# Unread matmuls in the tail of an attention and expert kernel, and an earlier second input load

## The reference

```python
# layer 1: linear cross-attention, 16 heads of depth 8
q, k, v = (split_heads(layernorm(z @ w) * gamma + beta) for z, w in ((h, wq), (ctx, wk), (ctx, wv)))
q_prime, k_prime = relu(q) + 1e-6, (relu(k) + 1e-6) * mask
kv = einsum('bhnd,bhne->bhde', k_prime, v * mask)
z = 1 / (einsum('bhnd,bhd->bhn', q_prime, k_prime.sum(-2)) + 1e-6)
out = layernorm(einsum('bhnd,bhde,bhn->bhne', q_prime, kv, z) @ dense_w + dense_b) * gamma + beta
# layer 2: causal self-attention (16 heads, softmax), then a mixture of 8 experts, top 2
h = h + attention(layernorm(h) * g1 + b1)
f = layernorm(h) * g2 + b2
w_full = softmax over the two largest of (f @ gate_W + gate_b), 0 elsewhere
h = h + sum_e w_full[:, e] * (gelu(f @ W1[e] + b1[e]) @ W2[e] + b2[e])
```

## Time and profile before

| | us |
|---|---|
| median of 3 runs | 579.07 (576.87 to 579.16) |
| the profiled execution, its own time | 577.21 |
| its span, first to last instruction | 575.4 |
| PE busy in the span | 492.3 (86%) |
| DVE busy | 400.5 (70%) |
| POOL busy | 326.4 (57%) |
| ACT busy | 284.0 (49%) |
| mean granted clock of PE | 0.93 |

### The profile page before, as it was taken

How to read it: one execution, slowest core, us unless ns; L and a number is a source line. 1 busy time by engine, 2 the same in 40 slices (tenths; PEclk the granted TensorE clock), 3 DMA queues, 4 the chain that set the end, 5 groups by cost and what they waited for, 6 DMA issues and landing times.

```text
span 575.4 us, 13859 instructions
## 1 busy us (share of the span) xinstructions
PE 492.3 (86%) x4469; PEld 405.7 (71%) x4469; DVE 400.5 (70%) x1239; ACT 284.0 (49%) x686; POOL 326.4 (57%) x349
## 2 busy tenths in 40 slices
PE   2998899999998999999999998942299999999920
PEld 2655578778777777777767866732299999999920
DVE  5775878999899899799799786425055555555536
ACT  2215338467466565565566555311166555656510
POOL 4625546557778778678768667345245545454520
PEclk9999899999999999999999999655599999999975
DMA  4920100100200200100000000001467777767639
GB/s 95 223 71 0 39 2 1 38 2 2 58 19 3 56 21 14 44 20 1 21 19 11 21 9 25 16 19 52 140 197 203 200 215 209 205 197 217 190 115 327
DMA packets 57851, 47.71 MB, mean 83 GB/s; under 512 B 15406, under 2 KB 44465, under 8 KB 57780
## 3 DMA queue, kind: packets, MB, share of 16 engines
q1 hardware_dynamic: 53460, 38.35, 24.5%
q0 software_dynamic: 4320, 8.47, 4.3%
HBM read 35.18 MB, written 12.08 MB: 82 GB/s over the span
## 4 chain that ended last, share of the span: by engine, by line
PE 45%; DVE 26%; issue 9%; POOL 8%; DVEq 4%; DMA 3%; ACT 2%; SPq 1%; POOLq 0%
PE bank L721 11%; PE bank L731 11%; POOL sorted_rows L1125 3%; PE bank L456 3%; PE bank L536 3%; DVE mx L1415 2%; DVE places L1383 2%; PE bank L563 2%; PE bank L541 2%; PE bank L373 2%; DVE places L1292 2%; POOL rs L989 2%; DVE vbd L1404 1%; PE bank L713 1%; DVE places L1288 1%
## 5 line engine op out<-in xcount | busy, mean ns | idle before, releaser
L1184 POOL DMA_INDIRECT result_rows<-back,rows x71 | 69.6, 980 | 77.1 <-DVE back L1641 74.9
L964 ACT ACTIVATE mid<-bank,b 128x128 f32<-128x128 f32 x284 | 81.2, 369 | 52.5 <-PE bank L721 52.5
L1125 POOL DMA_INDIRECT sorted_rows<-send,slot_u x64 | 64.1, 1002 | 29.2 <-issue 14.4
L1107 POOL TENSOR_TENSOR km<-kb,head 128x512 f32<-128x512 f32 x56 | 58.2, 1044 | 34.0 <-ACT kb L834 22.3
L721 PE MATMUL bank<-hT,w 128*128 128x128 f32 x568 | 76.7, 279 | 0.1
L731 PE MATMUL bank<-w,mid 128*128 x568 | 74.9, 275 | 0.0
L563 PEld LDWEIGHTS bank<-vbd,pT 128*128 128x128 f32 x512 | 65.4, 197 | 13.3 <-ACT pT L859 5.9
L721 PEld LDWEIGHTS bank<-hT,w 128*128 128x128 f32 x568 | 70.4, 195 | 0.6 <-issue 0.5
L563 PE MATMUL bank<-vbd,pT 128*128 128x36 f32 x512 | 66.6, 277 | 4.6 <-DVE places L1427 2.8
L731 PEld LDWEIGHTS bank<-w,mid 128*128 128x128 f32 x568 | 68.9, 192 | 0.0
L536 PE MATMUL bank<-km,qbd 128*128 128x512 f32 x128 | 67.8, 612 | 0.0
(11 more groups left out here) (204 smaller groups left out, 983.2 us busy)
## 6 DMA issues: line engine op xcount, KB each, us to landing
w<-in_L_ffn_exp_W_dram SPq DMA_DIRECT2D x79, 256.0 KB, 3.6
rows<-sorted_rows SPq DMA_DIRECT2D x71, 65.0 KB
places<-result_rows SPq DMA_DIRECT2D x16, 256.0 KB
places<-in_x_dram SPq DMA_DIRECT2D x8, 256.0 KB, 2.9
places<-in_ctx_dram SPq DMA_DIRECT2D x8, 256.0 KB, 3.4
out_dram<-acc SPq DMA_DIRECT2D x8, 256.0 KB, 5.8
result_rows<-back,rows POOLq DMA_INDIRECT x71, 3.0
sorted_rows<-send,slot_u POOLq DMA_INDIRECT x64, 2.4
```

Of the source, the lines that this page charges most:

```text
L964: A(mid[s][:, c, :], hidden[2 * s + c // 2][:, c % 2 * P:c % 2 * P + P], ACT.Gelu, bias=b1[:, bass.ds(expert, 1), c]).then_inc(mid_ok, 1)
L1107: G.tensor_tensor(km[n % 2][:, :, :], kb[u][:, n % 2, t * S:t * S + S].unsqueeze(1).broadcast_to([P, HG, S]), head8[:, :].unsqueeze(2).bro ...
L1125: G.indirect_dma_start(out=sorted_dram, out_offset=bass.IndirectOffsetOnAxis(ap=slot_u[u][:, j // 2, t:t + 1], axis=0), in_=send[u][:, t, ...
L1184: G.indirect_dma_start(out=result_dram, out_offset=bass.IndirectOffsetOnAxis(ap=rows[s][:, D:D + 1].bitcast(U32), axis=0), in_=back[s % 4] ...
```

## The change

It does two things. On PE, `keep_busy` gets a second argument, the bank to write. For the last group alone it is called with bank F1: twice ahead of the wait of `probs_values` in each of units 4 to 7 (unit 4 also waits for the last `kf_ok`, so that F1 is free), 3 times ahead of the wait of `y_T`, 20 ahead of `a_T`, 4 ahead of `gate_logits`, 6 ahead of `ranks`. After the count it is called 54 times ahead of the expert phase's first wait. On SP, `load(1, 1)` is moved ahead of the last 16 of the 18 other weights, behind the first two (`gamma_b` and `beta_b`). Both waits on `w_loaded` still ask for all 18.

```diff
-                for dst, src in other_weights:
+                for dst, src in other_weights[0:2]:
                     sp.dma_start(dst, src).then_inc(w_loaded, 16)
                 load(1, 1)
+                for dst, src in other_weights[2:]:
+                    sp.dma_start(dst, src).then_inc(w_loaded, 16)
...
-                def keep_busy(n):
+                def keep_busy(n, unread=probT_bank):
                     for _ in range(n):
-                        pe.matmul(probT_bank[:, :], ident_bf[:, :], causal[:, :].unsqueeze(1).broadcast_to([P, HG, S]),
+                        pe.matmul(unread[:, :], ident_bf[:, :], causal[:, :].unsqueeze(1).broadcast_to([P, HG, S]),
                                   start=True, stop=True)
...
                 def probs_values(k, n):
                     u, t = k % 2, n // 2
+                    if k == GROUPS - 1 and n >= 4:
+                        if n == 4:
+                            pe.wait_ge(kf_ok, GROUPS)
+                        keep_busy(2, F1)
                     pe.wait_ge(pT_ok, k * UNITS + n + 1)
...
                 def y_T(k):
+                    if k == GROUPS - 1:
+                        keep_busy(3, F1)
...
                 def a_T(k):
+                    if k == GROUPS - 1:
+                        keep_busy(20, F1)
...
                 def gate_logits(k):
+                    if k == GROUPS - 1:
+                        keep_busy(4, F1)
...
                 def ranks(k):
+                    if k == GROUPS - 1:
+                        keep_busy(6, F1)
...
+                keep_busy(54, F1)
                 pe.wait_ge(table_ok, 1)
```

## The result

| | before | changed |
|---|---|---|
| median of 20 runs, us | 581.81 (576.87 to 585.49) | 577.12 (572.86 to 580.26) |
| profiled execution, its own time, us | 577.21 | 577.16 |
| span, us | 575.4 | 575.4 |
| mean granted clock | 0.930 | 0.949 |

A forecast was written before the change was run, and what follows sets the result against it. The prediction took the kernel's tail to be a serial chain with PE steps at half clock. Terms −3.85 + 0.88 − 0.74 = −3.7 us, from a mean of 578.1, gave 574.4 us; range 570.4 to 578.5.

The forecast's parts named there:

- The clock through the tail: Five PE steps from the last unit's values to the gate run at full instead of half clock: −3.85 us.
- rival C: Clock falls again in mid-tail, before the second transposes, as most PE steps there are narrow: 577.2 us, chance 0.23.
- The pairs of units 4 and 5: Last group: four unread products where PE has no idle time push every later step: +0.88 us, bounds 0 and 1.76.
- the estimate of double: One unread product, 0.22 us at full clock, was taken to cost 0.44 us at half clock.
- upper bound of 1.76: Most that the four unread products in units 4 and 5 could cost, in us, if the clock is at half.
- The fillers fit in their waits: Tail: the 3, 20, 4, 6 and 54 unread products fit in PE's waits at full clock, costing 0.
- The start of the blocks: First expert blocks: the clock falls again in or behind the gap after the 54, so 0; bounds −1.3 and +1.5 us.
- The start: Group 0: SP's earlier loads remove only the idle time ahead of `key_sums`: −0.74 us, bounds −2.5 and 0.
- the bound of 0: Gain from SP's reordering is nothing if a weight lands late or a later stage gives it back.
- rival B: More than the sum: blocks start at full clock (573.1 us) or half clock around 359 to 368 us vanishes (570.4); chance 0.16.

The follow-up runs named there:

- The second: The changed kernel as it is, measured again on a chip where the kernel before has a median of 580.3 us: ratio 0.997 (0.9943 to 0.9996).

## Why the prediction was right, and where it was not

The forecast was a gain of 3.7 us. The first measurement gave 4.7 us (3.2 to 6.4 by the interval) and bears it out. The second gave 1.7 us (0.2 to 3.3), and 3.7 lies just outside it; the two lie on either side of the forecast. The first pair of profiles shows no gain at all, as their equal spans say: 2.2 us less in the tail, 2.7 more in the units, 0.3 more in the first blocks. The terms one by one:

- *The clock through the tail, −3.85 us.* The tail fell from 39.7 to between 35.8 and 36.1 us in five profiles, so −3.6 to −3.9. In three others the clock fell again at 390 to 392 us, just at the gate; there the tail took 37.3 to 38.6 us. This is rival C, with a later fall than it assumed, after `a_T`. It cost the gate's 1.05 us and the slower 6 products. I gave C 0.23; 3 of the 8 profiles with these fillers, away from the slower chip, show it. C leaned on the 9 us at half clock and said that PE was busy there with narrow steps. That reading was wrong: of the 10.2 us, some 3.2 went to products of 512 columns (L541 at 358.83 and 360.11, L534 and L536 from 365.56 to 367.65). So those 9 us don't show that the transposes are what kept the clock down.
- *The pairs of units 4 and 5, +0.88 us.* The units took 29.0 us instead of 28.2 in three profiles with the same 10.2 us at half clock: +0.8. Where the clock was at half for 13.7 us they took 30.9 to 31.0, +2.7 to +2.8. The pairs are not the cause of the longer stretch: on the slower chip it also came without them (29.8 us, against 31.0 with them). In the first profile the pairs ran at half clock and took 0.85 and 0.78 us each from their start to the next step's, as the estimate of double said. My upper bound of 1.76 covers the pairs but not the longer stretch.
- *The fillers fit in their waits, 0.* So it was at full clock: 0.24 to 3.2 us of idle time stayed behind all of them but the 4. The 4 ended together with ACT's copy (at 389.03 and 388.98 us in the changed kernel's second profile).
- *The start of the blocks, 0.* The clock fell behind the 54 in every profile with them, at 407 to 415 us (423 on the slower chip), and rose 3.4 to 6.8 us later (there 6.8 to 10.2). The first blocks took 7.2 to 8.6 us instead of 7.1 (there 7.2 and 8.8). The 54 had left 1.35 to 3.2 us idle ahead of the first rows (there 5.8 to 6.0), and the second rows brought a further wait of 1.2 to 1.4. With 66, which left 0.5 us ahead of the first rows and the same 1.25 ahead of the second, it did not fall, nor with 67, which left nothing; the first blocks took 6.5 and 5.8 us. The Trainium skill, "TensorE: Matmul & The Clock Gate", section "Loop structure matters more than you think", has matmuls behind a long wait for a transfer run cold; the trace agrees, with 3.4 to 6.8 us at half clock behind the 54. So the term of 0 was about right for the first blocks. What it left out is the slower chip, where the profiles with the 54 have the first rows some 2.5 us later.
- *The start, −0.74 us.* This is the weakest step. I let PE's 32 products begin where they did before, so I put the gain at `key_sums` at 0.74 us, and I took it as kept to the end. Locally it was larger: 1.2 us in the profile run again, 2.0 in the first one, 1.7 with SP's order alone. The last two had luck in them, the earlier first rise of the clock. At the end SP's order alone is worth 0.9996 (0.9966 to 1.0026). That is nothing by its middle, but the interval holds 0.74 us as well. The profiles speak against a gain that is kept: in none of the eight with the loads moved does the first exponential of the last group start more than 0.4 us earlier than before (344.0 us), and in four it starts 0.9 to 1.9 us later. So the bound of 0, that a later stage gives it back, looks like the right case.

So the gain is that of the tail: the unread products alone give 0.9953 (0.9918 to 0.9987), and the forecast of the tail's terms alone was 0.9949. The mechanism of the main term held. That the total came out near the forecast is in part luck, as it holds 0.74 us for the start that the runs don't show, and the two measurements are 3 us apart. The rest of the first one, 4.7 against 2.7 us, lies within the intervals and is not explained further.

What caused the half clock around 360 us was left as chance in rival B. It is PE's 1.67 us wait for DVE ahead of unit 2: with six products in that wait the fall is gone in both profiles, and the units take 23.7 instead of 28.2 us. That is 4.5 us, the some 4 us that rival B priced, and the changed kernel's pairs in units 4 to 7 come after it. The median fell by 5.7 us from the changed kernel's; the units account for 5.3 of it, of which 0.8 are the pairs of units 4 and 5 taken out.

## What to carry to other kernels

Unread matmuls pay where PE is on the chain and would run it at half clock, and where they fit in a wait that is already there. Put them in the wait that the fall of the clock follows, not in the busy stretch behind it. If they are to hold the clock for the next work, they must reach nearly to the end of the wait: the 54 that left 1.35 to 3.2 us open did not. Count them for half clock too: the 67 came late where the clock had fallen ahead of them. And try each burst by taking it out, on more than one chip: on the slower one the two kernels with the 54 show no gain, and the one without them shows 4.5 us (0.9924). A shift of 2 us at the start of a pipelined kernel is no gain until it is seen at the end; follow one step of each group through the trace.

## What the runs showed of the hardware that I had not expected

- The clock falls behind short waits. PE had waited 1.67 us ahead of the fall at 358.5 us. The falls of 3.4 us at 64.9 and 228.8 us in the profile of before, and those at 62.7, 185.5 and 270.9 us with SP's order alone, come 1.7 to 2.7 us behind PE's wait of 1.0 to 1.4 us for DVE ahead of `key_sums` (the first line is of the profile of before, the second of SP's order alone):

```profile
62.21 1.05 PE L440 MATMUL bank<-emb,places 128*128 128x2 f32 x8 [1.37 <-DVE places L1292]
182.85 1.05 PE L442 MATMUL bank<-emb,places 128*128 128x2 f32 x8 [1.09 <-DVE places L1294]
```

The same wait comes without a fall in other groups (1.09 us ahead of 184.6 us and 0.98 ahead of 269.9 in the profile of before). What decides is not shown.

- Once the clock also fell in dense work. In the profile of six ahead of unit 2 it was at half for 6.8 us from 291.1 us, and PE had been busy for 7.94 us of the 8.00 ahead:

```profile
283.00:291.00 8.00, 7.94 (x58) 6.62 (x57) 6.72 (x27) 6.06 (x12) 5.26 (x7) 1.00 0.06 20
291.10:297.90 6.80, 6.80 (x23) 4.82 (x22) 5.77 (x27) 1.46 (x3) 4.89 (x5) 0.50 0.06 20
```

- PE can be busy all the time and stay at half clock for 10.2 to 13.7 us (9.00 of 9.00 us, 13.00 of 13.00 in the profile after). Its steps there are transposes and products of 8, 36 and 512 columns.
- The same kernel takes 595.8 us on one chip and 580.3 to 581.8 on others. The difference builds up in the groups, where PE pauses with nothing in the trace that releases it, and where the stretches at half clock add up to 20.5 to 27.3 us ahead of the last group's units, against 6.8 to 17.1 in the others. Why is not shown.
